# Experts computed only on rows sent to them, in one iteration with the attention of the same batch, in a fused audio-tower kernel

## The chip, the cores and the metric

The kernel runs on one core of a Trainium2 chip, all in fp32. The metric is device time in microseconds (us) from start to end of one execution; lower is better. The engines are called as the profile calls them: PE (TensorE, matmuls and transposes), DVE (VectorE), ACT (ScalarE), POOL (GpSimd) and SP (SyncE, which here issues the DMAs). Each has its own instruction queue and takes it strictly in order; they meet at semaphores.

## What is computed

The reference, cut to what matters, for x of 32 batches of 80000 samples:

```python
f = dct(frames_of_128(x))                         # 626 frames of 128 per batch (the last one is zero)
xo = concat(mamba2(f, fwd), flip(mamba2(flip(f), bwd))) @ proj_W.T + proj_b
h1 = layernorm(f + xo)                            # selective scan: 4 heads of 64, state 16, both directions

# what follows is wrapped in  h = h + block(layernorm(h)):
p = softmax(u @ gate_w + gate_b); top_w, top_idx = top_k(p, 2)                    # mixture of 8 experts
moe = sum_e gate[t, e] * (gelu(u @ w1[e] + b1[e]) @ w2[e] + b2[e])                # w1 128x512, w2 512x128
att = softmax over 8 following tokens of (q[t + w] + pos[w]) * k[t], times v[t + w]     # per channel
ffn = pattern FFN: top 64 of 512, then top 128 of 256, then top 64 of 512 activations kept
```

The gate is zero for the six experts that a token has not chosen.

## The kernel before, in words

A batch is 626 tokens, held as 5 tiles of 128 (`TILES`, `W` = 640). Three stages work on three different batches in one iteration of a loop: stage 1 (DCT, both Mamba2 directions, layer norm) on batch b, stage 2 (experts, then windowed attention) on b−1, stage 3 (the top-k FFN) on b−2. `run` writes two iterations ahead of the loop, 30 in it and two behind it. The order of the work inside an iteration is written out by hand: each engine has a string (`PE_ORDER`, `ACT_ORDER`, `DVE_ORDER`, `POOL_ORDER`), and each digit of it says whose stage's next step is emitted there; a step ends at a `yield`. SP has no string: per iteration it loads x, stores the output `hk` (L266, L267) and spreads the decays (L273, L279).

Stage 1 has 12 windows of 121 rows (6 chunks, 2 directions). For each, DVE runs a scan over the decays (L904) on a buffer of a ring of four (`ab0` to `ab3`), which SP fills from `decay_rows` in HBM by a broadcast load (L279), and multiplies (L912, L915); PE computes around it (L491, L501, L507, L527). At its end POOL does the last steps of the layer norm (L348, L311, L353, L356) and `h = h + u` (L359).

Stage 2 takes moments of h on DVE (L863, L866, L868, L869), POOL normalizes (L311, L316), PE and DVE compute the gate (L951 to L968). All eight experts then run on all 640 tokens, with their weights in SBUF for the whole program: 64 matmuls for the first layer (L574, each 128 hidden units by 320 tokens), ACT's gelu on each (L778), and 160 matmuls (L585) for the second, in 10 groups of four outputs. DVE first adds the product of gates and b2 (L973), then each output times its gate: 40 operations at L982. The attention follows: q, k, v on PE, eight products on DVE (L992), maxima (L995 to L998), POOL subtracts (L370), ACT exponentiates 128x5120 (L794), POOL sums trees (L376, L381, L385, L390, L399), DVE multiplies (L1003), takes a reciprocal (L1007) and the last product `kf` (L1010); PE transposes it, DVE adds it (L1013).

Stage 3 is DVE's largest: for every tile and each of three lists, rounds of MAX (eight largest, L1038) and MATCH_REPLACE (L1040), then masks (L1049, L1078), with PE's transposes and matmuls between; the last matmul of a tile (L682) is added to `hk` on DVE (L1060). `hk` is first filled with a copy of h by POOL (L408). Each first MAX on a1 waits for PE's matmul and ACT's gelu (L804) of that tile. Two tick instructions (L314, L1031) are 1 element wide.

PSUM has 8 banks of 128x512: `pS` (stage 1) three, `pM` (stage 2) three, `pD` (stage 3) two. Two small pieces show the form of the order:

```python
def merged(order, *stages):
    for digit in order:
        stage = stages[int(digit) - 1]
        if stage is not None:
            next(stage, None)
```

## Time and profile before

| | us |
|---|---|
| median of 3 runs | 8677.74 |
| lowest to highest | 8659.9 to 8679.93 |
| profiled execution, its own time | 8673.34 |
| its span | 8670.7 |
| PE busy | 6907.8 (80%) |
| DVE busy | 7915.2 (91%) |
| ACT busy | 3389.3 (39%) |
| POOL busy | 2524.6 (29%) |
| granted PE clock, mean | 0.809 of full speed |

Busy times are of one profiled execution, and the sum of a prediction is made against that execution's own time. The span counts from the first to the last instruction. DVE's share is a mean over the whole program; the loop has the same 262 us pattern 30 times, so one iteration, and the seam between two of them, can be read for all.

### The profile page before, as it was taken

How to read it: one execution, taken by the hardware profiler on the slowest of the kernel's cores; microseconds unless marked ns; L12 is line 12 of the kernel's file. 1: busy time of each engine (PE TensorE's matmuls, PEld its weight loads, DVE VectorE, ACT ScalarE, POOL GpSimd, SP SyncE). 2: the span in 40 equal slices, each digit the busy share in tenths (PEclk: the TensorE clock that was granted, in tenths of full speed). 3: DMA queues.
4: the chain of work that ended last, by engine and by line, in shares of the span. 5: the costliest groups of instructions: out<-in, count | busy, mean ns of one | idle time of the engine just before them, and what ended most of it. 6: DMA issues, size and time to landing. Idle time of an engine off the chain costs nothing.

```text
span 8670.7 us, 114685 instructions
## 1 busy us (share of the span) xinstructions
PE 6907.8 (80%) x35336; PEld 5042.4 (58%) x35336; DVE 7915.2 (91%) x23276; ACT 3389.3 (39%) x5803; POOL 2524.6 (29%) x2481
## 2 busy tenths in 40 slices
PE   6788887788878788878788887888878888777863
PEld 4566565566655565655565655566655656555642
DVE  2699999999999999999999999999999999999998
ACT  2344433344433344433344433444333444333431
POOL 1332123332133332233322233321233322333320
PEclk8788877788877788877888877888877888777875
DMA  1000000000000000000000000000000000000000
GB/s 57 15 17 15 8 12 17 17 17 15 7 13 17 17 16 14 10 13 17 17 15 10 10 17 17 17 15 8 12 17 17 17 15 7 13 17 17 14 2 3
DMA packets 95339, 128.48 MB, mean 15 GB/s; under 512 B 7600, under 2 KB 94096, under 8 KB 94096
## 3 DMA queue, kind: packets, MB, share of 16 engines
q1 hardware_dynamic: 94736, 120.71, 5.0%
q8 instruction: 345, 5.65, 0.3%
q14 instruction: 258, 2.11, 0.1%
HBM read 109.68 MB, written 11.01 MB: 14 GB/s over the span
## 4 chain that ended last, share of the span: by engine, by line
DVE 55%; PE 32%; issue 5%; POOL 4%; ACT 3%; DMA 1%; DVEq 0%; SPq 0%; POOLq 0%; ACTq 0%
DVE m L1038 17%; DVE work L1040 15%; PE pM L585 9%; PE pM L574 7%; DVE a L1040 4%; DVE ab L904 3%; PE pS L507 2%; DVE hid L992 2%; ACT hid L778 2%; DVE h L982 2%; PE pS L473 2%; DVE stats L863 2%; PE pS L501 2%; DVE a L1049 2%; PE pS L527 1%
## 5 line engine op out<-in xcount | busy, mean ns | idle before, releaser
L1040 DVE MATCH_REPLACE8 work<-m,work 128x256 f32<-128x256 f32 (+1 forms) x4192 | 2156.0, 522 | 0.0
L1038 DVE MAX8 m<-work 128x8 f32<-128x256 f32 (+1 forms) x4192 | 2014.0, 526 | 1.0
L574 PE MATMUL pM<-uT,cst 128*128 128x320 f32 x4096 | 1473.2, 480 | 179.5 <-DVE h L973 117.3
L311 POOL TENSOR_TENSOR rstd<-vare,mhalf 128x5 f32<-128x5 f32 x160 | 187.5, 1172 | 4671.2 <-DVE vare L869 4671.1
L778 ACT ACTIVATE hid<-pM,cst 128x320 f32<-128x320 f32 x2048 | 1061.6, 528 | 1031.2 <-PE pM L574 685.8
L585 PEld LDWEIGHTS pM<-cst,hid 128*128 128x128 f32 x10240 | 1191.9, 193 | 184.6 <-DVE h L982 110.8
L585 PE MATMUL pM<-cst,hid 128*128 128x128 f32 x10240 | 1219.2, 277 | 97.9 <-DVE h L982 97.2
L574 PEld LDWEIGHTS pM<-uT,cst 128*128 128x128 f32 x4096 | 690.5, 199 | 758.5 <-ACT hid L778 533.2
L473 PE MATMUL pS<-u_fm,wconv_s 128*128 128x315 f32 (+1 forms) x3072 | 861.3, 432 | 0.0
L507 PE MATMUL pS<-Mt,Xw 121*64 121x121 f32 x3072 | 377.9, 392 | 492.1 <-DVE Mt L915 492.1
L473 PEld LDWEIGHTS pS<-u_fm,wconv_s 128*128 128x128 f32 (+1 forms) x3072 | 496.1, 167 | 347.5 <-issue 92.9
L904 DVE TENSOR_TENSOR_SCAN ab<-ab,cst 121x488 f32<-121x488 f32 x384 | 614.4, 1606 | 32.3 <-DMA ab<-decay_rows 32.2
L370 POOL TENSOR_TENSOR hid<-hid,red 128x640 f32<-128x640 f32 x256 | 387.4, 1548 | 809.1 <-DVE red L998 809.1
L752 ACT COPY xs<-pS 128x242 f32<-128x242 f32 x384 | 138.9, 362 | 1171.5 <-PE pS L507 1171.5
L507 PEld LDWEIGHTS pS<-Mt,Xw 121*64 121x64 f32 x3072 | 245.9, 201 | 571.9 <-DVE Mt L915 526.8
L1038 DVE MAX8 m<-a 128x8 f32<-128x512 f32 x768 | 504.3, 677 | 38.4 <-issue 38.2
L982 DVE SCALAR_TENSOR_TENSOR h<-pM,lgt,h 128x128 f32<-128x128 f32 x1280 | 358.5, 343 | 130.7 <-PE pM L585 120.6
L399 POOL TENSOR_TENSOR hid<-hid 128x640 f32<-128x640 f32 x224 | 393.0, 1778 | 130.2 <-DVE hid L1003 125.1
L501 PE MATMUL pS<-xs,skip 128*128 128x121 f32 x1536 | 359.7, 379 | 14.7 <-ACT xs L752 14.7
L1040 DVE MATCH_REPLACE8 a<-m,a 128x512 f32<-128x512 f32 x512 | 345.3, 674 | 0.0
L677 PE MATMUL pD<-cst,a 128*128 128x128 f32 x640 | 146.4, 372 | 248.8 <-DVE a L1049 171.7
L831 ACT COPY selT<-pD 128x512 f32<-128x512 f32 x160 | 93.4, 584 | 638.8 <-PE pD L677 638.8
(195 smaller groups left out, 11986.4 us busy)
## 6 DMA issues: line engine op xcount, KB each, us to landing
ab<-decay_rows SPq DMA_DIRECT2D x384, 230.7 KB
x_sb<-in_x SPq DMA_DIRECT2D x32, 256.0 KB
out<-hk SPq DMA_DIRECT2D x32, 256.0 KB
cst<-in_weights SPq DMA_DIRECT2D x2, 2048.0 KB, 12.0
hid<-in_setup SPq DMA_DIRECT2D x1, 1904.0 KB, 20.9
out<-hk SPq DMA_DIRECT2D x32, 57.0 KB
x_sb<-in_x SPq DMA_DIRECT2D x32, 56.5 KB
cst<-in_weights SPq DMA_DIRECT2D x1, 1344.0 KB, 17.0
```

Source lines behind the costliest of these rows:

```text
L370: last = nc.gpsimd.tensor_tensor(lg[:, w, :], lg[:, w, :], red[:, 0, :], ALU.subtract)
L399: last = nc.gpsimd.tensor_tensor(lg[:, w, :], lg[:, w, :], lg[:, w + n, :], ALU.add)
L473: last = nc.tensor.matmul(pS[0:rows, 512 * (n % 3):512 * (n % 3) + HQ], wt, tap(d, i, half * HQ, HQ), start=(j == 0), stop=(j == len(block ...
L501: nc.tensor.matmul(pS[:, B2 + g * WIN:B2 + (g + 1) * WIN], skip[:, 2 * d + g, :], xs[d][:, g, NS + ch * WIN:NS + (ch + 1) * WIN], start=(g ...
L507: last = nc.tensor.matmul(pS[r * HD:(r + 1) * HD, B2 + g * WIN:B2 + (g + 1) * WIN], Xw[d][:, hh, :], Mt[d][:, hh, :], start=False, stop=(g ...
L574: nc.tensor.matmul(pM[:, 512 * (n % 2):512 * (n % 2) + W // 2], w1[:, e, j * P:(j + 1) * P], uT[:, lo:lo + W // 2], start=True, stop=True) ...
L585: last = nc.tensor.matmul(pM[:, B2 + P * (m % 4):B2 + P * (m % 4 + 1)], hid[:, e % 2, j, tok(t)], w2[:, e, j, :], start=(j == 0), stop=(j ...
L778: nc.scalar.activation(hid[:, e % 2, j, lo:lo + W // 2], pM[:, 512 * (n % 2):512 * (n % 2) + W // 2], ACT.Gelu, bias=c("b1")[:, n // 2:n / ...
L904: nc.vector.tensor_tensor_scan(decays, decays, c("scan_src", WIN), 0.0, ALU.mult, ALU.add).then_inc(G["scanned"].s, 1)
L982: last = nc.vector.scalar_tensor_tensor(h2[:, t, :], pM[:, B2 + P * (m % 4):B2 + P * (m % 4 + 1)], gate[:, t, e:e + 1], h2[:, t, :], ALU.m ...
L1038: link(nc.vector.max(m[i], now[i]), len(tiles) - 1)
L1040: link(nc.vector.match_replace(work[i], m[i], now[i], GONE), len(tiles) - 1 if r or firsts is None else 0)
```

## The change

Four stages with the lags 0, 1, 1 and 2: stage 2 is now routing and experts, stage 3 the attention **of the same batch in the same iteration**, stage 4 the top-k FFN. Three batches are in flight, as before. The experts run only on the rows sent to them:

1. DVE marks the two chosen experts of each token, PE counts with two matrices of constants (`before`, `ones`) how many earlier rows chose the same expert (`rank_ps`), and DVE makes of this a slot for each row, experts following one another in whole tiles of 128 rows, and the expert of each of the 17 tiles (`MT` = 2·5 + 8 − 1).
2. POOL scatters the normalized rows to `routed_rows` in HBM with ten indirect DMAs (L463), SP loads them back as tiles (L334) and reads the 17 expert numbers into registers (L372), with which it loads each tile's expert (w1, w2, b1, b2 in one DMA of 128x1156, 592 KB, L327) into a ring of three.
3. For each tile PE does 4 up matmuls, one for the bias, 4 down, and the transpose of the tile after the next; ACT does 4 gelus of 128x128 and a copy of answer and transpose together (`keep`). SP stores the answers to `answer_rows` (L341), POOL gathers them by ten indirect DMAs (L471), and DVE adds them to h2 into h3, times their weights, in ten operations (L1143, L1146).
4. SP gets an order of its own. The decay loads (L316), the expert loads and the row loads now stand in one queue.
5. Attention has a bank of its own, `pA`; `pM` shrinks to two. Its q, k and v go one after the other through that bank, and its transposes go in 4 + 1 tiles. h, h2 and h3 are separate buffers, as are un and u3. POOL's h2 = h + u (L453) waits for `moe_done` of the batch before, and the hk copy (L518) is moved to the end of the attention, directly ahead of it.
6. The experts' weights (4 MB) are not loaded ahead any more; `routed_rows` is zeroed once at the start.

The diff, cut to its core:

```diff
+MT = 2 * TILES + E - 1
+WR = 3
+EC = 4 * P + KB * P + KB + P
+STAGE_LAG = (0, 1, 1, 2)
...
-POOL_ORDER = ("321132222222221121111")
+POOL_ORDER = ("214211412131133333333331")
+SP_ORDER = ("1212122222222222311311222112212222122222244")
...
+        def sp_stage2(sp, b):
...
+            which = expert_of_tiles(sp)
+
+            def weights(i):
+                sp.wait_ge(G["tile_done"].s, G["tile_done"](b, max(i + 1 - WR, 0)))
+                sp.dma_start(expert[i % WR][:], experts_d[bass.ds(which[i], 1), :, :].rearrange("o p c -> p (o c)")).then_inc(G[f"expert{i % WR}"].s, 16)
...
+            for i in range(WR):
+                weights(i)
+            yield
+
+            sp.wait_ge(scattered.s, scattered(b, 160))
+            sp.wait_ge(G["moe_done"].s, G["moe_done"](b, 0))
+            routed(0)
+            routed(1)
+            for i in range(MT):
+                if i + WR < MT:
+                    yield
+                    weights(i + WR)
+                if i % 4 == 1 and i // 4 + 2 < GROUPS:
+                    yield
+                    routed(i // 4 + 2)
+                if i % 2 == 1 or i == MT - 1:
+                    yield
+                    answers(i // 2)
...
         def pool_stage2(pool, b):
+            normalized(pool, 1, 1, b, un, h2).then_inc(G["u2_done"].s, 1)
+            yield
+
+            pool.wait_ge(G["u2_done"].s, G["u2_done"](b, 1))
+            pool.wait_ge(G["slots_done"].s, G["slots_done"](b, 1))
+            nc.gpsimd.tensor_tensor(ticks[:, 0:1], zero1[:, 0, :], zero1[:, 0, :], ALU.add)
+            for k in range(2 * TILES):
+                nc.gpsimd.indirect_dma_start(routed_d, bass.IndirectOffsetOnAxis(ap=slot[:, k:k + 1], axis=0), un[:, k % TILES, :], None,
+                                             bounds_check=MT * P - 1, oob_is_err=False).then_inc(scattered.s, 16)
+            yield
+
+            pool.wait_ge(G["y_out0"].s, G["y_out0"](b, 80))
+            pool.wait_ge(G["y_out1"].s, G["y_out1"](b, 64))
...
+            for k in range(2 * TILES):
+                nc.gpsimd.indirect_dma_start(rows[:, k, :], None, answers_d, bass.IndirectOffsetOnAxis(ap=slot[:, k:k + 1], axis=0),
+                                             bounds_check=MT * P - 1, oob_is_err=False).then_inc(gathered.s, 16)
...
+            def up(i):
...
+                for j in range(KB):
+                    last = nc.tensor.matmul(pM[:, bank(i) + j * P:bank(i) + (j + 1) * P], w1_of(i, j), turned[:, (i + 2) % 4, 1, :],
+                                            start=True, stop=True)
+                last.then_inc(G["hid_ps"].s, 1)
+
+            def down(i):
...
+                nc.tensor.matmul(at, c("ones", 1), b2_of(i), start=True, stop=False)
+                for j in range(KB):
+                    last = nc.tensor.matmul(at, hid[:, i % 2, j, :], w2_of(i, j), start=False, stop=(j == KB - 1))
+                if i + 2 < MT:
+                    last = turn(i + 2)
+                last.then_inc(G["tile_done"].s, 1)
...
-                for m in range(4 * i, 4 * i + 4):
-                    e, t = divmod(m, TILES)
-                    last = nc.vector.scalar_tensor_tensor(h2[:, t, :], pM[:, B2 + P * (m % 4):B2 + P * (m % 4 + 1)], gate[:, t, e:e + 1],
-                                                          h2[:, t, :], ALU.mult, ALU.add)
...
+            for t in range(TILES):
+                last = nc.vector.scalar_tensor_tensor(h3[:, t, :], rows[:, t, :], top8[:, t, 0:1], h2[:, t, :], ALU.mult, ALU.add)
+            link(last)
+            for t in range(TILES):
+                last = nc.vector.scalar_tensor_tensor(h3[:, t, :], rows[:, TILES + t, :], top8[:, t, 1:2], h3[:, t, :], ALU.mult, ALU.add)
+            last.then_inc(G["moe_done"].s, 1)
```

**SP's queue from the output store or x on to the first decay loads.** In these rows buffer numbers are left out; a name in brackets is the semaphore waited for, and ISA or REGISTER_ALU rows are waits and registers. Before:

```order
L266 ISA [waits out_sb]
L266 DMA out<-hk 128x4x128
L267 ISA
L267 DMA out<-hk 114x128
L272 ISA [waits dA_sb]
L273 DMA decay_rows<-dAT 48x122 [waits scanned]
L279 DMA ab<-decay_rows 121x488 [waits m_done,dA_out]
L279 DMA ab<-decay_rows 121x488 [waits m_done] x3
```

After, the third expert load to the fourth tile's:

```order
L327 DMA expert<-in_experts 128x1156
L305 REGISTER_ALU
L306 ISA [waits dA_sb]
L307 DMA decay_rows<-dAT 48x122 [waits scanned]
L334 DMA rows<-routed_rows 128x4x128 [waits moe_done,scattered]
L334 DMA rows<-routed_rows 128x4x128
L316 DMA ab<-decay_rows 121x488 [waits m_done,dA_out]
L316 DMA ab<-decay_rows 121x488 [waits m_done] x3
L327 ISA [waits tile_done]
L327 DMA expert<-in_experts 128x1156
```

The two row loads and their wait for the scatters now stand between the decays' store and the first decay load, and expert loads stand among the decay loads; the output store has gone to the end of the iteration.

**DVE's queue at the seam between two iterations.** `ub_t` is stage 1's sum, `pD` the output of the FFN. Before:

```order
L866 BN_AGGR mv<-stats 128x2 [waits link1]
L866 BN_AGGR mv<-stats 128x2 x4
L868 TENSOR_SCALAR nmean<-mv 128x5 [waits link1]
L869 TENSOR_SCALAR vare<-mv 128x5
L1060 TENSOR_TENSOR hk<-hk,pD 128x128 [waits fin_ps,sel3]
L1060 TENSOR_TENSOR hk<-hk,pD 128x128 [waits fin_ps]
L1097 ISA
L301 COMPARE_AND_BRANCH
L863 BN_STATS stats<-h 128x6 [waits u4_done,h1_done]
```

After (`lg` is the attention's weighted values, `pA` its transposes, `h` here stands for h3 up to the branch):

```order
L1177 TENSOR_TENSOR kf<-lg,red 128x640 [waits val_tree]
L1180 TENSOR_TENSOR h<-h,pA 128x512 [waits attT_ps]
L1229 TENSOR_TENSOR hk<-hk,pD 128x128 [waits fin_ps,sel3]
L1184 TENSOR_TENSOR h<-h,pA 128x128 [waits attT_ps]
L1016 BN_STATS stats<-h 128x6 [waits h3_done]
L1021 TENSOR_SCALAR nmean<-mv 128x5 [waits link3]
L1022 TENSOR_SCALAR vare<-mv 128x5
L1229 TENSOR_TENSOR hk<-hk,pD 128x128 [waits fin_ps]
L380 COMPARE_AND_BRANCH
L1016 BN_STATS stats<-h 128x6 [waits h1_done]
```

Before, the last rows of an iteration were stage 1's, and the attention lay inside it; now the last product of the attention, its two additions and its moments come last, and the first rows of the next iteration take moments of h2 as before.

**POOL's queue at the same place, after.** `un` and `u` are normalized rows, `vare` the variances:

```order
L510 TENSOR_TENSOR lg<-lg 128x640 [waits val_tree]
L404 TENSOR_TENSOR rstd<-vare,mhalf 128x5 [waits var3]
L407 TENSOR_TENSOR tick_pool<-zero 128x1 [waits rstd3]
L409 TENSOR_SCALAR u<-h,nmean,rstd 128x128 x5
L517 ISA [waits h3_done]
L518 TENSOR_TENSOR hk<-h,zero 128x640 [waits out_dma]
L453 TENSOR_TENSOR h<-h,u 128x640 [waits moe_done,attn_scaled]
L380 COMPARE_AND_BRANCH
L404 TENSOR_TENSOR rstd<-vare,mhalf 128x5 [waits var2]
L407 TENSOR_TENSOR tick_pool<-zero 128x1 [waits rstd2]
L409 TENSOR_SCALAR un<-h,nmean,rstd 128x128 x5
L461 TENSOR_TENSOR ticks<-zero 128x1 [waits slots_done,u2_done]
L463 DMA routed_rows<-un,slot 2176x128 x10
```

Before, stage 1's layer norm and `h = h + u` ended POOL's iteration and the hk copy opened the next one, alone; now the attention's last sum, u4, the hk copy and h2 stand in a row, and the ten scatters (last row) follow behind the normalization.

## Rows read from the trace of the kernel before

**Rows 1.** The page's part 1: busy time and share of the span, xinstructions.
```profile
PE 6907.8 (80%) x35336; PEld 5042.4 (58%) x35336; DVE 7915.2 (91%) x23276; ACT 3389.3 (39%) x5803; POOL 2524.6 (29%) x2481
```

**Rows 2.** The page's part 4: the chain that ended last, by engine.
```profile
DVE 55%; PE 32%; issue 5%; POOL 4%; ACT 3%; DMA 1%; DVEq 0%; SPq 0%; POOLq 0%; ACTq 0%
```

**Rows 3.** Windows: length, busy time of each engine, PEclk, DMA share, GB/s.
```profile
608.00:4010.00 3402.00, 2787.32 (x14318) 2038.55 (x14316) 3201.41 (x9436) 1379.25 (x2350) 1016.50 (x995) 0.82 0.05 14
4272.00:8200.00 3928.00, 3212.47 (x16513) 2347.97 (x16514) 3695.38 (x10900) 1593.27 (x2712) 1174.56 (x1152) 0.82 0.05 14
```

**Rows 4.** Instructions of line L359, start and end of the span: min/median/max ns, starts in us.
```profile
L359 POOL TENSOR_TENSOR h<-h,u x3: 1530/1530/1533, 141.1 to 634.6; 128x640 f32<-128x640 f32 x3
...
L359 POOL TENSOR_TENSOR h<-h,u x3: 1532/1532/1533, 7718.0 to 8243.6; 128x640 f32<-128x640 f32 x3
```

**Rows 5.** Instructions of line L408.
```profile
L408 POOL TENSOR_TENSOR hk<-h,zero x32: 1248/1252/1257, 375.6 to 8489.7; 128x640 f32<-128x640 f32 x32
```

**Rows 6.** Timeline of DVE at the seam: start us, us, instruction [idle before <-releaser].
```profile
4041.55 0.29 DVE L1060 TENSOR_TENSOR hk<-hk,pD 128x128 f32<-128x128 f32 x1 [3.16 <-PE pD L682]
4046.27 1.07 DVE L863 BATCH_NORM_STATS2 stats<-h 128x6 f32<-128x128 f32 x5 [4.43 <-POOL h L359]
...
4048.77 0.69 DVE L1038 MAX8 m<-a 128x8 f32<-128x512 f32 x1 [0.68 <-issue]
```

**Rows 7.** Groups of DVE, 4010 to 4272: xcount | busy us, mean ns | idle before.
```profile
L904 DVE TENSOR_TENSOR_SCAN ab<-ab,cst 121x488 f32<-121x488 f32 x12 | 19.3, 1617 | 0.0
...
L982 DVE SCALAR_TENSOR_TENSOR h<-pM,lgt,h 128x128 f32<-128x128 f32 x40 | 11.2, 342 | 1.7 <-PE pM L585 1.5 <-DVE a L1049 0.2
...
L973 DVE TENSOR_TENSOR h<-h,pM 128x640 f32<-128x640 f32 x1 | 0.8, 810 | 0.0
...
L967 DVE TENSOR_TENSOR lgt<-lgt,top 128x40 f32<-128x40 f32 x2 | 0.4, 200 | 0.1
```

**Rows 8.** Instructions of line L904 (scans), first iteration and a steady one.
```profile
L904 DVE TENSOR_TENSOR_SCAN ab<-ab,cst x12: 1165/1168/1175, 78.0 to 109.0; 121x488 f32<-121x488 f32 x12
...
L904 DVE TENSOR_TENSOR_SCAN ab<-ab,cst x12: 1146/1563/2191, 4206.0 to 4265.7; 121x488 f32<-121x488 f32 x12
```

**Rows 9.** The page's part 5: PE groups.
```profile
L574 PE MATMUL pM<-uT,cst 128*128 128x320 f32 x4096 | 1473.2, 480 | 179.5 <-DVE h L973 117.3
...
L585 PE MATMUL pM<-cst,hid 128*128 128x128 f32 x10240 | 1219.2, 277 | 97.9 <-DVE h L982 97.2
...
L507 PE MATMUL pS<-Mt,Xw 121*64 121x121 f32 x3072 | 377.9, 392 | 492.1 <-DVE Mt L915 492.1
```

**Rows 10.** Windows of 10 us, PE alone: length, busy, PEclk, DMA share, GB/s.
```profile
3994.00:4004.00 10.00, 10.00 (x50) 0.50 0.29 79
...
4094.00:4104.00 10.00, 10.00 (x76) 1.00 0.00 0
```

**Rows 11.** The page's part 6: line, engine, xcount, KB each, us to landing.
```profile
cst<-in_weights SPq DMA_DIRECT2D x2, 2048.0 KB, 12.0
```

**Rows 12.** Waits of SP's queue: us in total, times, longest us.
```profile
SPq L279 <- DMA decay_rows<-dAT: 30.5, 32, 1.5
...
SPq L124 <- DMA out<-hk: 1.8, 1, 1.8
```

**Rows 13.** Timeline of SP's queue, first iteration.
```profile
74.39 1.49 SPq L279 DMA_DIRECT2D ab<-decay_rows  x4
```

**Rows 14.** Instructions of three POOL lines: min/median/max ns.
```profile
L314 POOL TENSOR_TENSOR tick_pool<-zero x160: 192/193/194, 45.4 to 8472.5; 128x1 f32<-128x1 f32 x160
...
L311 POOL TENSOR_TENSOR rstd<-vare,mhalf x160: 1164/1175/1192, 44.1 to 8471.2; 128x5 f32<-128x5 f32 x160
...
L348 POOL TENSOR_TENSOR rstd<-vare,mhalf x32: 1960/1960/1971, 127.8 to 8228.7; 128x10 f32<-128x10 f32 x32
```

**Rows 15.** Timeline of POOL, attention of one iteration.
```profile
3959.01 12.01 POOL L370 TENSOR_TENSOR hid<-hid,red 128x640 f32<-128x640 f32 x8 [25.43 <-DVE red L998]
...
4001.10 12.49 POOL L399 TENSOR_TENSOR hid<-hid 128x640 f32<-128x640 f32 x7 [4.12 <-DVE hid L1003]
4013.56 1.65 POOL L339 TENSOR_TENSOR yg<-xs,zs 128x525 f32<-128x525 f32 x2
```

485 lines of the change are left out of this document (290 added, 195 removed).

## The prediction

> **What bounds the kernel now.** I read the page first. VectorE (DVE) is busy 91% of the span, the matmul engine (PE) 80%, ScalarE (ACT) 39%, GpSimd (POOL) 29% [rows 1], and the chain that ended last runs 55% on DVE and 32% on PE [rows 2]. Two windows of whole steady iterations hold 3201.41 us of DVE work in 3402 and 3695.38 in 3928 [rows 3]: 94.1% busy. The loop's period comes from the starts of an instruction that runs once per iteration, POOL's h += u (L359): there are 29 periods between 634.6 and 8243.6 [rows 4], **262.4 us** each. So DVE works 246.9 us of an iteration and stands idle 15.5. The timeline of the seam between two iterations shows about half of that idle time: 3.16 us for the last output matmul, 4.43 for POOL's h, 0.68 more [rows 6], together 8.3; the other 7.2 lie in small waits. What the change is worth is what it does to these 246.9 and 15.5.
>
> **DVE work that goes and comes.** In one iteration [rows 7] the 40 accumulations of expert outputs (L982) are 11.2 us, the first sum with b2 (L973) 0.8, the two gate products (L967) 0.4. In come ten accumulations of L982's form, 2.8; eleven small operations for the slots and the expert table, at most 160 wide, at 0.2 to 0.25 each like L967's, 2.6; and 0.3 because h3's sum is split in two. Adding up all rows of the loop in both orders with the trace's durations gives −7.1: 246.9 becomes 239.8.
>
> **Scans.** The twelve scans are 19.3 us of an iteration [rows 7], each from 1.15 to 2.19; in the first iteration, where POOL does nothing beside them, all take 1.17 [rows 8]. Below, a DVE row's position is the sum of the durations of the rows ahead of it in the changed loop. The scans stand at positions 44 to 121, when POOL has issued its ten scatters and waits for the answers; its attention passes come later. I take 12 × (1.60 − 1.17) = 5.2 off: 234.6. The lower bound of this gain is nothing, should the indirect DMAs or the attention passes slow DVE wherever they land.
>
> **PE and ACT.** L574 and L585 took 1473.2 + 1219.2 us over 32 batches [rows 9], 84.1 per iteration. In their place stand 17 tiles of 10 matmuls or transposes of 128x128, at L585's 1219.2/5120 = 0.238 each: 40. DVE, not PE, sets the end, so I count none of the 44 as gain; it is slack. [...] One tile's expert is 592 KB; 2048 KB took 12.0 us [rows 11], so a load takes 3.5 to 5 us; 17 are 60 to 85 us of an iteration, three in flight. I cost them at nothing: the tiles' own PE time and the mixes between them cover that; without that cover each tile past the third would wait up to 2 us.
>
> **Waits that come.** (a) SP: the decay loads (L316) now stand behind the wait for all ten scatters. The slots are ready at DVE position 26.9. With p the price of one indirect DMA on POOL, scan 0 is ready at 26.9 + 10p + 2 (landing; 1.5 and 1.8 in [rows 12]) + 0.8 for two issues + 3.5 from a decay load's issue to its scan (74.39 [rows 13] to 78.0 [rows 8]) = 44.9 at p = 1.17, with the DVE at 43.8; with semaphores I say 2 us late.
> (b) POOL: the gather follows the last answers' store and must be in by position 154.8. It starts 12.7 us after the last combine; 5.3 us are left at p = 1.17, none at p = 1.7.
> (c) The trace has no indirect DMA. **p** is bounded by POOL's small instructions: 0.19 (128x1 add) below and 1.96 (pow on 128x10) above [rows 14]. I take 1.17, the pow on 128x5, as nearest to an instruction that reads one column of 128 and starts something for each. [...]
> (d) PE between expert tiles and mixes: both stand in its one queue. Mix 0 is ready near 75 and DVE is there at 72 to 73. Over the mixes, tiles 5 to 14 (10 × 2.23 at full clock) and twelve windows at 2.0 (L507 alone 377.9/384 = 0.98 at a mean clock of 0.8 [rows 9]) are 46 us of PE beside 45.8 of DVE. I charge 1. Idle inside the iteration: 7.2 + 2 + 1, about **10**.
> (e) The seam: a batch's attention now ends where the iteration does. kf waits for POOL's tree; that chain ran from 3959.01 to 4013.59 [rows 15], 54.6 us with its own waits, 45 to 50 of it work, against 46.4 of DVE work laid beside it: 3. The transposes into pA: 0.9. Then u4's moments, POOL's pow (1.17) and five scalings (1.1 to 2.2), PE's transposes, ACT's copy, a1's matmul, ACT's table and gelus stand in a row before the next iteration's first MAX: 11, with 2 of DVE work beside. POOL's hk copy (1.25) and h2 (1.53) queue there too, behind the store of the batch before (0.7 of issue, 1.8 of landing [rows 12]), 5.3 in all, hidden in those 11. Sum **13**, against 8.3.
>
> **Sum.** 234.6 + 10 + 13 = 257.6. A walk like this misses waits and invents none, so I add 1.4: **259** per iteration. The first iteration ended at 141.1 [rows 4], the second at 375.6 [rows 5]: I take 133 (4 MB of weights less to load ahead) and 226 (no experts' DVE work, 7 less). Iteration 32 took 8489.7 − 8243.6 = 246 and becomes 222, since nothing of experts and attention is left in it; the last stays near 183. With 2.6 around the span: 133 + 226 + 30 × 259 + 222 + 183 + 2.6 = **8537**, say 8540. The profiled run took 8673.34, 0.05% under the runs' median of 8677.74; no shift is made.
>
> **Rivals.**
> **A, slower**: an indirect DMA costs its upper bound. At p = 1.96 scan 0 is 7.9 us later and the gather 2.6 late: +10.5, 269.5 per iteration, 8852. It decides from a loss of 4.7 on, p about 1.64. For: sending 128 rows is more work than a pow on five columns. Against: an issue need not wait for its landing. Chance 0.22.
> **B, slower**: PE's work is now short bursts between three engines, and it is granted 0.50 where the expert part had 1.00 [rows 10]. The 46 us of (d) become 92, PE sets the pace there, and the period is near 300: 9700. For: the clock is at 0.50 in other parts. Against: PE has no longer gaps there than before. Chance 0.05.
> **C, no change**: in (d) each tile waits for ACT and each mix for DVE, in one queue; 0.4 us at each of twelve mixes is 5 per iteration, 8690. For: L507 already sat 492 us waiting for DVE's Mt [rows 9]. Chance 0.13.
> **D, faster**: waits overlap, and idle stays at 15.5: 250 per iteration, 8270. For: (a) and (e) take independent work beside them. Against: seam work is one chain. Chance 0.13.
> **E, it doesn't do what it says**: half of PE's work on experts goes and the time doesn't move, since the chain is 55% DVE's [rows 2]. That is how I read it, and it is in each case above: the gain comes from DVE's 12 us, not from PE's 44.
>
> **How the numbers follow.** Forecast 0.47, A 0.22, B 0.05, C 0.13, D 0.13. A measurement of this kernel tells about 0.3% (26 us) from no change. Faster by more: forecast, D and 0.02 of C, 0.62. Within: 0.10 of C. Slower: A, B and 0.01 of C, 0.28. The range runs from 8330 to 8890: it holds the forecast, C, A by rows, and the nearer half of D; B and the rest of D, some 0.15, are left out.
>
> **What would show it.** POOL's h2 (L453) at a period of 259 with DVE busy 234 to 236 of it; scans near 1.2; indirect DMAs 1.2 us apart; DVE waiting some 2 us for ab0; a seam idle near 13, behind kf, pA and a1. It would be wrong with DMAs 1.6 us apart or more and long waits for ab0 or the gather (A), with PEclk 0.5 between scan 0 and scan 11 (B), with waits of 0.4 us or more at every mix (C), or with DVE's work not falling.

## The result, and the profile after

The changed kernel takes 8774.64 us (median of 4 runs, 8771.2 to 8786.13) beside 8678.83 for the kernel before (4 runs, 8659.9 to 8688.26): a ratio of **1.0117**, 95% interval 1.0103 to 1.0132. It is slower by 1.2%, where 1.6% faster was forecast. The profiled run took 8773.84 us, its span 8771.9. One execution of e15_head_early (below) took 10598 us at a mean granted clock of 0.533; it lies outside the range given there and outside the ratio.

The page's busy time by engine, answering to [rows 1]:

```profile
PE 6056.2 (69%) x31240; PEld 4389.9 (50%) x31240; DVE 7622.0 (87%) x22604; ACT 3284.6 (37%) x6696; POOL 2994.0 (34%) x3187
```

The change does what it says: DVE's work fell by 293 us (7915.2 to 7622.0) and PE's by 852. The time rose by 96, so DVE stands idle longer. The chain that ended last, answering to [rows 2], shows DMA and POOL where PE had been:

```profile
DVE 60%; PE 13%; DMA 9%; issue 8%; POOL 7%; ACT 2%; SPq 1%; POOLq 0%; DVEq 0%; ACTq 0%
```

**The period.** POOL's h2 (L453) runs once per iteration:

```profile
L453 POOL TENSOR_TENSOR h<-h,u x32: 1530/1532/1543, 134.3 to 8338.8; 128x640 f32<-128x640 f32 x32
```

The first two starts are 134.3 and 372.9, the third 638.7; (8338.8 − 638.7)/29 is 265.5 us per iteration, forecast 259, before 262.4. Two windows inside the loop, answering to [rows 3] (length, then busy time of PE, PEld, DVE, ACT, POOL, then PEclk, DMA share, GB/s):

```profile
700.00:4094.00 3394.00, 2389.34 (x12479) 1737.18 (x12477) 3046.89 (x9022) 1308.82 (x2662) 1193.32 (x1260) 0.75 0.22 65
4360.00:8300.00 3940.00, 2804.40 (x14582) 2035.28 (x14582) 3538.03 (x10524) 1544.04 (x3129) 1371.00 (x1461) 0.75 0.22 66
```

These windows are not whole numbers of iterations. Over the 29 whole ones (length, DVE busy, PEclk, DMA share, GB/s):

```profile
638.70:8338.80 7700.10, 6901.02 (x20474) 0.75 0.22 65
```

6901.02 / 29 is **238.0 us of DVE work in an iteration, and 27.5 us idle**. Before it was 246.9 and 15.5. So 8.9 us of work went and 12.0 of idle time came.

**Where DVE waits.** DVE's waits over the same 29 iterations of both kernels (what waited, for what: us in total, times, longest). After, 639 to 8339:

```profile
DVE ab L1057 <- DMA ab<-decay_rows: 227.5, 87, 6.0
DVE stats L1016 <- POOL h L453: 176.3, 29, 6.3
DVE stats L1016 <- ACT h L837: 163.8, 29, 7.4
DVE kf L1177 <- POOL lg L510: 41.5, 29, 1.4
DVE hk L1229 <- PE pD L814: 38.6, 29, 1.5
DVE h L1180 <- PE pA L741: 37.1, 29, 1.3
DVE Xw L1065 <- PE pS L602: 34.1, 34, 3.0
```

Before, 635 to 8243:

```profile
DVE stats L863 <- POOL h L359: 121.3, 29, 4.7
DVE hk L1060 <- PE pD L682: 99.3, 29, 4.0
DVE h L982 <- PE pM L585: 45.5, 63, 1.2
DVE m L1038 <- issue: 34.5, 29, 2.1
...
DVE ab L904 <- DMA ab<-decay_rows: 0.8, 2, 0.4
```

In these rows "issue" stands where the trace shows nothing that the engine waited for. Divide by 29. Scans waiting for their decays went from 0 to **7.8 us** per iteration, at three scans of twelve (87 waits in 29 iterations); the wait for h2 from 4.2 to 6.1; the wait for the next batch's h (L837) is new, **5.6**. kf, pA and hk together are 4.0, hk alone was 3.4. That is 16 us more. In return the small waits of the list before are nearly gone, among them 1.6 for the expert matmuls (L982 <- PE) and 1.2 for the first MAX (L1038). The difference is the 12 us.

**The seam** in DVE's timeline at 4085, answering to [rows 6] (start, us, instruction, idle before):

```profile
4085.04 0.69 DVE L1180 TENSOR_TENSOR h<-h,pA 128x512 f32<-128x512 f32 x1 [1.28 <-PE pA L741]
...
4089.90 0.29 DVE L1229 TENSOR_TENSOR hk<-hk,pD 128x128 f32<-128x128 f32 x1 [1.47 <-PE pD L814]
4096.12 1.07 DVE L1016 BATCH_NORM_STATS2 stats<-h 128x6 f32<-128x128 f32 x5 [5.93 <-POOL h L453]
...
4103.30 1.07 DVE L1016 BATCH_NORM_STATS2 stats<-h 128x6 f32<-128x128 f32 x5 [5.36 <-ACT h L837]
```

With 1.4 for kf and 0.4 for L1184 that is 15.8 idle, where the forecast had 13. POOL's and PE's rows say why:

```profile
4089.95 2.18 POOL L409 TENSOR_SCALAR u<-h,nmean,rstd 128x128 f32<-128x128 f32 x5
4093.34 1.25 POOL L518 TENSOR_TENSOR hk<-h,zero 128x640 f32<-128x640 f32 x1 [1.21 <-DMA out<-hk]
4094.55 1.53 POOL L453 TENSOR_TENSOR h<-h,u 128x640 f32<-128x640 f32 x1
```

```profile
4092.18 1.12 PE L750 MATMUL pA<-cst,u 128*128 128x128 f32 x4 [2.32 <-POOL u L409]
4094.05 0.47 PE L754 MATMUL pA<-cst,u 128*128 128x128 f32 x1 [0.75 <-ACT u4T L950]
4098.12 1.32 PE L545 MATMUL pS<-cst,x_sb 128*128 128x128 f32 x5 [3.59 <-DMA x_sb<-in_x]
```

u4 is ready at 4092.13. POOL waits 1.21 for the out store, copies hk, and only then adds h2. PE turns u4, comes to the loop's end, and 3.59 us later turns the *next* batch's x; ACT copies it, PE does the DCT, ACT copies h, and DVE goes on at 4103.30. The forecast had put the adding of h2 inside the 11 us of a1's chain, and had no term for h.

**The scans and the masks.** DVE's groups from 700 to 8300, shapes kept apart. After:

```profile
L1057 DVE TENSOR_TENSOR_SCAN ab<-ab,cst 121x488 f32<-121x488 f32 x347 | 405.7, 1169 | 221.5 <-DMA ab<-decay_rows 221.5
L1218 DVE SCALAR_TENSOR_TENSOR a<-work,a 128x512 f32<-128x512 f32 x228 | 219.2, 961 | 5.7
L1247 DVE SCALAR_TENSOR_TENSOR a<-work,a 128x256 f32<-128x256 f32 x145 | 80.9, 558 | 0.0
```

Before:

```profile
L904 DVE TENSOR_TENSOR_SCAN ab<-ab,cst 121x488 f32<-121x488 f32 x348 | 560.7, 1618 | 0.8 <-DMA ab<-decay_rows 0.8
L1049 DVE SCALAR_TENSOR_TENSOR a<-work,a 128x512 f32<-128x512 f32 x230 | 157.8, 686 | 5.8
L1078 DVE SCALAR_TENSOR_TENSOR a<-work,a 128x256 f32<-128x256 f32 x145 | 60.5, 417 | 1.0
```

A scan fell from 1618 to 1169 ns, 5.4 us per iteration against 5.2 forecast. But the masks that read two tiles now stand beside POOL: 686 became 961 ns (2.2 us per iteration), 417 became 558 (0.7). At 4077.83 and 4079.62 L1218 took 1.73 and 1.89 us while POOL's tree (L510) ran beside it; of its 256 instructions 62 took over 0.9 us, and every one of them lay beside L510.

**The indirect DMAs** in POOL's timeline:

```profile
4130.77 0.97 POOL L463 DMA_INDIRECT routed_rows<-un,slot  x1 [0.30 <-issue]
4132.05 0.97 POOL L463 DMA_INDIRECT routed_rows<-un,slot  x1 [0.31 <-issue]
```

These are the second and third of ten. They stand 1.28 us apart (the first, at 4129.35, 1.42 ahead), near the 1.17 taken and far from rival A's 1.64. The gathers stand 1.31 apart and land 2.6 after issue.

### The profile page after: what moved, and what is told of

Same layout as the page of the kernel before. It is cut to its first block, busy times and chain, and to the rows that moved or that the text cites. A ratio compares the mean times of both kernels' runs of the same rounds, so it can differ in the third digit from the quotient of the medians.

```text
span 8771.9 us, 110100 instructions
## 1 busy us (share of the span) xinstructions
PE 6056.2 (69%) x31240; PEld 4389.9 (50%) x31240; DVE 7622.0 (87%) x22604; ACT 3284.6 (37%) x6696; POOL 2994.0 (34%) x3187
## 4 chain that ended last, share of the span: by engine, by line
DVE 60%; PE 13%; DMA 9%; issue 8%; POOL 7%; ACT 2%; SPq 1%; POOLq 0%; DVEq 0%; ACTq 0%
DVE m L1207 19%; DVE work L1209 19%; DMA ab<-decay_rows 5%; POOL lg L510 4%; DVE a L1209 3%; DVE lg L1159 2%; POOL routed_rows L463 2%; PE pM L704 2%; PE pM L693 2%; DMA x_sb<-in_x 2%; PE pS L584 1%; DVE ab L1057 1%; DVE Mt L1068 1%; DVE stats L1016 1%; DVE lg L1170 1%
## 5 line engine op out<-in xcount | busy, mean ns | idle before, releaser
L584 PE MATMUL pS<-u_fm,wconv_s 128*128 128x315 f32 (+1 forms) x3072 | 974.7, 470 | 41.3 <-ACT Cs L868 40.8
L906 ACT ACTIVATE hid<-pM,expert 128x128 f32<-128x128 f32 x2176 | 622.7, 371 | 384.2 <-PE pM L693 382.3
L1057 DVE TENSOR_TENSOR_SCAN ab<-ab,cst 121x488 f32<-121x488 f32 x384 | 449.0, 1169 | 295.8 <-DMA ab<-decay_rows 295.7
L704 PE MATMUL pM<-expert,hid 128*128 128x128 f32 x4352 | 652.4, 295 | 0.0
L693 PE MATMUL pM<-turned,expert 128*128 128x128 f32 x4352 | 602.2, 283 | 40.8 <-ACT turned L915 38.1
L481 POOL TENSOR_TENSOR lg<-lg,red 128x640 f32<-128x640 f32 x256 | 383.5, 1536 | 662.0 <-DVE red L1165 662.0
L693 PEld LDWEIGHTS pM<-turned,expert 128*128 128x128 f32 x4352 | 539.6, 194 | 89.9 <-issue 64.5
L704 PEld LDWEIGHTS pM<-expert,hid 128*128 128x128 f32 x4352 | 545.9, 197 | 67.3 <-issue 3.1
L510 POOL TENSOR_TENSOR lg<-lg 128x640 f32<-128x640 f32 x224 | 362.6, 1643 | 160.9 <-DVE lg L1170 155.7
L814 PE MATMUL pD<-cst,selT 128*128 128x128 f32 x1280 | 328.4, 437 | 108.0 <-ACT selT L984 108.0
L814 PEld LDWEIGHTS pD<-cst,selT 128*128 128x128 f32 x1280 | 281.7, 324 | 171.4 <-ACT selT L984 171.4
L471 POOL DMA_INDIRECT rows<-answer_rows,slot x320 | 323.6, 1011 | 105.0 <-issue 105.0
```

What stands on the lines that cost most here:

```text
L471: nc.gpsimd.indirect_dma_start(rows[:, k, :], None, answers_d, bass.IndirectOffsetOnAxis(ap=slot[:, k:k + 1], axis=0), bounds_check=MT * P ...
L481: last = nc.gpsimd.tensor_tensor(lg[:, w, :], lg[:, w, :], red[:, 0, :], ALU.subtract)
L510: last = nc.gpsimd.tensor_tensor(lg[:, w, :], lg[:, w, :], lg[:, w + n, :], ALU.add)
L584: last = nc.tensor.matmul(pS[0:rows, 512 * (n % 3):512 * (n % 3) + HQ], wt, tap(d, i, half * HQ, HQ), start=(j == 0), stop=(j == len(block ...
L693: last = nc.tensor.matmul(pM[:, bank(i) + j * P:bank(i) + (j + 1) * P], w1_of(i, j), turned[:, (i + 2) % 4, 1, :], start=True, stop=True)
L704: last = nc.tensor.matmul(at, hid[:, i % 2, j, :], w2_of(i, j), start=False, stop=(j == KB - 1))
```

## The experiments

All edits are to the changed kernel, and ratios are to the kernel before, timed on the same chip. Waits are totals of DVE from 700 to 8100, about 28 iterations. The theory at the start was that three waits ate the gain, each made by the order of a queue. So three orders were moved, one at a time and together. Where a time "after L453" is given, it is the median over the 29 iterations of that run's trace.

**e1_x_early.** SP loads the next x before it waits to store out.

```diff
-SP_ORDER = ("1212122222222222311311222112212222122222244")
+SP_ORDER = ("142121222222222223113112221122122221222222")
-            run(sp, SP_ORDER, sp_stage1, sp_stage2, idle, sp_stage4)
+            run(sp, SP_ORDER, sp_stage1, sp_stage2, idle, sp_stage4, lags=(0, 1, 1, 3))
```

> SP loads x of the next batch ahead of the output store, as before the change, and not behind it. Theory (x sits behind a store that waits for the iteration's last DVE operation): DVE's wait for ACT's h (L837), 5.6 us per iteration, falls to under 2.5, the rest being POOL's h2 that ACT's copy of x waits for; the period falls from 265.5 by 3 to 5.5, the time by 90 to 165 us to 8610-8685. Rival (the wait only moves to the first MAX or to scan 0, because the seam is bound by POOL's h2 and the decays come late anyway): period within 1 of 265.5, time within 30 of 8775.

8842.2 us, 1.0183 [1.0165, 1.0201]. The theory fell: DVE's wait for h stayed at 5.7 us per iteration. The trace also shows something the edit can't cause: engines stood before instructions for which nothing was missing, as `ACT xs L871 <- remote` for up to 6.3 us, and single register operations of SP of up to 0.71.

**e2_decays_first.** SP issues the decay loads ahead of the wait for scattered rows (the fourth and fifth step of its order):

```diff
-SP_ORDER = ("1212122222222222311311222112212222122222244")
+SP_ORDER = ("1211222222222222311311222112212222122222244")
```

> On SP the four first decay loads go ahead of the wait for the scatters and of the two row loads. Theory (queue order makes scan 0 late): the wait for ab0, 3 to 4.6 us in an iteration, falls to under 1, the period by 2.5 to 4, the time by 75 to 120 us to 8655-8700; the waits for later decays (some 3 us per iteration) stay. Rival (it is the traffic of the expert loads, which come out of the queue just ahead): ab0's wait stays over 2.5 and the time within 40 of 8775.

8992.0, 1.0356 [1.0339, 1.0373]. This theory fell too: DVE's scans still wait, and a new wait stands behind them.

```profile
DVE ab L1057 <- DMA ab<-decay_rows: 232.4, 82, 7.0
...
DVE tick L1200 <- ACT a L964: 120.3, 19, 7.6
DVE best L1207 <- ACT a L964: 49.9, 8, 7.9
```

The expert rows now leave SP behind the decays. PE's queue has the first tile's transposes ahead of the feed-forward matmuls (L772, L780) that make `a` for ACT's L964; the tile starts 61.5 us after L453 instead of 52.3, and DVE's top-k waits for `a`. The edit was not tested alone, though: in this run, as in e1, the last decays are copied 50.9 us after L453 and not 45.9, so that the first decay load left at 52.5, later than the 50.1 that it was to beat. e14 repeats the order without that delay.

**e3_h2_first.** POOL adds h2 ahead of the hk copy.

```diff
-POOL_ORDER = ("214211412131133333333331")
+POOL_ORDER = ("214211412131133333333133")
```

> POOL adds h2 = h + u in the gap ahead of u4 and not behind the copy to hk. Theory: DVE's wait for h2 at the seam, 6.1 us, goes, but x is loaded as late as before, so that the wait for h (L837) grows from 5.6 to 9 to 11 and the gain is only 0.5 to 2 us per iteration, 15 to 60 us: 8715-8760. Rival (the seam is POOL's h2 alone): the whole 6 us are gained, period 259.5, 8595.

8879.2, 1.0225 [1.0208, 1.0242].

```profile
DVE stats L1016 <- ACT h L837: 232.6, 27, 10.0
DVE stats L1016 <- issue: 78.0, 27, 3.1
```

The wait for h2 is gone, and the same idle time stands before the next thing: 8.6 us per iteration for h and 2.9 of "issue", 11.5 together, as much as both waits had been. The 2.9 is DVE's own loop end, which the wait for h2 had covered. Here, too, scans wait 284.5 us in all, with no edit near them: this run is of e1's set, and has its stalls.

**e4_all_three.** The three edits together.

> The three edits together. Theory: the waits are in different places of one chain per iteration, and x early together with h2 early frees both seam waits: 5.6 + 4 of 6.1 + 3.5 at ab0, 10 to 13 us per iteration of which the first MAX's wait takes back 2 to 4: period 255 to 257.5, time 8450 to 8530, below the kernel before (8679) by 1.7 to 2.6%. Rival (what is freed at the seam comes back at the decays, the gather and PE's mixes): period 260 or more, 8600 or more.

9028.7, 1.0397 [1.038, 1.0415]. No part had paid, and the three together did not either.

**e5_control.** The changed kernel unedited, among the next set of runs.

> The changed kernel, unedited, once more. Theory (the four edits really made it slower, by 2.5 to 8.5 us per iteration, because engines stalled on their next instructions around the first expert loads, which the first run of this kernel did not show): period 265.5 and 8775 again, within 0.3%, with no wait of that kind on ACT's L871. Rival (such stalls come and go with the load of a program or the session, whatever the edit): over 8810, with stalls of up to 6 us on ACT L871 and SP's first expert load 42 us or more after h2 and not 39.

8768.7, 1.0109 [1.0092, 1.0126], period 265.5, none of e1's stalls. The result repeats. Its scans wait 212.5 us in all; DVE waits 170.1 for h2 and 156.8 for h. These are the base of the comparisons below.

**e6_thin_experts.** Is it the experts' traffic that makes decays late? This kernel loads 128 of an expert's 1156 columns and leaves out the rest, so the experts' values are not those of the reference.

```diff
-                sp.dma_start(expert[i % WR][:], experts_d[bass.ds(which[i], 1), :, :]...
+                sp.dma_start(expert[i % WR][:, 0:P], experts_d[bass.ds(which[i], 1), :, 0:P]...
```

> Each expert load brings only the first 128 of its 1156 columns, 64 KB for 578 KB; the rest of w1 and all of w2 and the biases are left at zero, so the experts' values are left out; every instruction, wait and order stays. Theory (queue order and PE's half-clock projections make the decays late, not traffic): the wait for ab falls by 1 to 2.5 of 7.8 us per iteration since loads land a little faster, the seam's 6.1 and 5.6 stay, time 8700 to 8745. Rival (17 x 578 KB per iteration are what delays decay loads, row loads and answers): the wait for ab falls under 3 and the time to 8640 or less.

8732.5, 1.0072 [1.0055, 1.0089].

```profile
DVE ab L1059 <- DMA ab<-decay_rows: 163.1, 58, 5.0
```

The scans' wait falls from 212.5 in 83 places to 163.1 in 58, 7.6 to 5.8 per iteration, and the period from 265.5 to 263.9. The experts' traffic costs less than 2 us, and none of it at scan 0, which starts 55.8 us after L453 in both. From the first decay load to scan 0 it is 5.6 us in both as well; where the decay loads leave ahead of the two row loads it is 3.5 (e2) to 3.9 (e14). So the 2 us on top of the 3.5 forecast are the two row loads of 256 KB that leave just ahead.

**e7_pool_busy.** Thirty adds of 128x640 on POOL beside the scans.

```diff
+            for k in range(30):
+                pool.wait_ge(G["spare_done"].s, G["spare_done"](b, k))
+                nc.gpsimd.tensor_tensor(spare[:], ..., ALU.add)...
```

> POOL does 30 additions of 128x640 to a spare buffer behind the scatters, beside the scans and where it was idle. Theory (the scans are 1.17 and not 1.62 us only because POOL is idle beside them): the scans that fall beside these additions, 8 to 10 of 12, take 1.5 to 2.2 us, mean 1.45 to 1.65 over all; DVE's work rises by 3.5 to 6 us per iteration, the time by 80 to 250 us. Rival (scans are short because they stand singly between other DVE work, or for where the buffers lie): mean stays 1.17 and the time within 30.

8867.0, 1.0226 [1.0209, 1.0243]. The page's group of scans:

```profile
L1061 DVE TENSOR_TENSOR_SCAN ab<-ab,cst 121x488 f32<-121x488 f32 x384 | 521.8, 1359 | 202.1 <-DMA ab<-decay_rows 202.1
```

1169 became 1359 ns by POOL's work alone, less than the 1450 expected, because only a third of the scans lay beside an added POOL instruction: those 129 took 1.72 us in the mean, the 253 clear of it 1.17. That POOL's quiet makes scans short is shown. The masks pay the same price here (L1218 of the changed kernel, 960 ns in e5):

```profile
L1222 DVE SCALAR_TENSOR_TENSOR a<-work,a 128x512 f32<-128x512 f32 x226 | 306.7, 1357 | 5.7
```

DVE's MAX of 128x512, which reads one tile, is not stretched: 0.68 us beside the added instructions and clear of them.

**e8_all_three_thin.** e4 with e6's loads.

> The three edits of the fourth run, with the thin expert loads (experts' values left out). Theory (what the three edits lost they lost to stalls of SP, ACT and PE on their next instructions beside the burst of three expert loads): without the burst the stalls go, and the seam and the order give what was expected: period under 262, time under 8650, below both e6 and e4 by over 1%. Rival (the row loads behind the decays and the order itself are the loss, 4.6 us at the first MAX after scan 0): within 1% of e4, over 8930.

8889.2, 1.0249 [1.0232, 1.0266], no stalls. The scans' wait is down to 56.4 (2.1 per iteration), and the waits for `a` (L966 there) are 103.0 + 95.5, 7.3 per iteration. So the wait before the top-k that e2 brought is the order of the rows, neither the experts' traffic nor stalls: behind the four decay loads the first row load lands 7.0 us after its issue, here with thin experts as in e2 with whole ones, and 2.8 in the changed kernel.

**e9_x_early_again.** e1's kernel, unchanged, in another set of runs.

> The first experiment's kernel once more, since the control ran without any stall on instructions while the four edited kernels of the earlier set all had them. Theory (the stalls belong to that set of runs, or to where the programs lay then, and not to the edit): no register operation of SP over 0.2 us, first expert load 39 us after h2, decays from ACT at 46 us, period 265 to 265.6, time 8755-8785: no gain, since PE's first matmul after the loop's jump starts at 3.4 us either way. Rival (the edit shifts the code, and the stalls come with it): 8820 to 8850 again with SP's slow register operations up to 0.7 us.

8778.0, 1.0114 [1.0097, 1.013], with no stalls. e1's extra 64 us belonged to its set of runs, and e2 to e4 ran in that set: their ratios overstate, their waits' places stand. x early gains nothing by itself. PE's wait before L545 changes its name only, from the x load to "issue":

```profile
PE pS L545 <- issue: 100.4, 28, 4.9
```

That is 3.6 us per iteration for PE's jump to the loop's head.

**e10_x_and_h2.** e1's and e3's edits.

> x loaded ahead of the store and h2 added ahead of u4, the decay loads as in the changed kernel. Theory: from DVE's last output addition to its moments of h there are now 5.9 + 1.9 + 5.4 us; with x and h2 both ready, what is left is the jump of the loop (2.9 us on DVE, 3.4 on PE) and PE's two steps and ACT's two copies behind it, some 9 us, so the seam's idle falls by 3 to 4 us: period 261.5 to 263, time 8650 to 8700. Rival (DVE's h waits for PE's jump and u4's transposes, which follow DVE's last addition as before): period over 264.5, time over 8740.

8819.6 (8780.7 to 8824.8), 1.0151 [1.0122, 1.018]. The seam's idle time stays (238.4 for h, 77.5 "issue", 11.7 us per iteration), so the rival held: what h waits for is PE's place in its queue and the jump. The time is even 42 us above e9's in the medians, and the trace says where from. DVE's work is 239.3 us per iteration instead of 238.0, all of it in one instruction, kf (824 ns in e9):

```profile
L1177 DVE TENSOR_TENSOR kf<-lg,red x32: 825/2137/2141, 363.9 to 8615.6; 128x640 f32<-128x640 f32 x32
```

h2 added early is added beside kf, at 31 of 32 kfs. e3, e12 and e15 pay these 1.3 us too.


**e11_hint.** The jump back at the loop's end is announced by one more instruction in each engine's loop; the trace calls it BRANCH_PREFETCH_HINT and puts it at the head (39 ns on DVE).

```diff
-            with engine.Fori(last, NB) as b:
+            with nc.Fori(last, NB, engines=[engine.engine], hint_back_edge=True) as b:
```

> [...] Theory (a part of the seam is the jump itself, 3.4 us on PE ahead of its first matmul on x, and 2.9 on DVE): PE's jump hides nothing of x's load, which lands at the same time, so the gain is only 0 to 1 us per iteration: 8735-8775. Rival (the jump is hidden anyway or the announcement does nothing): the same within 15 us; and if it moves the code so that stalls come, 8800 or more.

8749.2, 1.008 [1.0063, 1.0096], against 1.0114 for e9 among the same runs. DVE's rows of the loop's end, from 700 to 8100, in this run:

```profile
L380 DVEq COMPARE_BRANCH  x28: 77/77/78, 897.6 to 8060.1; - x28
L380 DVEq BRANCH_PREFETCH_HINT  x28: 39/39/39, 898.2 to 8060.7; - x28
```

In the changed kernel:

```profile
L380 DVEq COMPARE_BRANCH  x28: 72/72/72, 903.4 to 8073.1; - x28
L380 DVEq FUSED_REGOPS  x28: 51/51/51, 906.5 to 8075.9; - x28
```

From the branch to DVE's next row it is 2.9 us there (median of 30) and 0.5 here. How the hint does that no trace shows. The wait for h is 140.8 instead of 157, that for h2 stays (175.2).

**e12_x_h2_hint.** e10 and e11.

> x early, h2 early and the jump announced, together. Theory (after x and h2 the jump is the seam's next limit): DVE goes to h2's moments within 0.5 us and PE starts on x within 1 us of the jump, so the seam loses 3 us more than with x and h2 alone: period 258.5 to 260.5, time 8560 to 8620, 0.7 to 1.4% below the kernel before. [...]

8731.7 (8706.9 to 8738.2), 1.0051 [1.0032, 1.0071].

```profile
DVE stats L1016 <- ACT h L837: 223.6, 28, 11.3
...
DVE stats L1016 <- issue: 16.7, 28, 0.6
```

DVE's jump goes from 2.9 to 0.6 us, PE's from 3.6 to 0.8. Against e10 the seam's idle time falls by the 3 us expected (11.7 to 8.6), and the time by 88. But e10 had not brought its own part: against the changed kernel 43 us are gained where 155 to 215 were expected, since h itself is still last, 8.0 per iteration.

**e13_decays_unit4.** The decays are computed and copied four at a time, so the last is ready sooner (`DA_UNIT = 8` becomes `4`).

> PE transposes the decays after 4 half projections and not after 8, some 8 us earlier, and ACT copies them as much earlier; SP's queue stays. Theory (two things hold scan 0 at the same time: the decays, copied at 45.9 us after h2, and on SP the wait for the scatters and two row loads, 49 to 50): alone it gains little, ab0's first load goes out at 49.5 to 50.2 as before, because the scatters end at 47.7: time 8745-8785, within 0.3% of 8770. Rival (the decays alone hold it): scan 0 2 to 4 us earlier, 8640 to 8710.

8779.1, 1.0115 [1.0092, 1.0139]. The last copy ends 40.8 us after L453 instead of 45.9, as expected without a gain: the first decay load still leaves at 50.4 (50.1 before), for it stands behind the wait for the scatters and SP's first row loads.

**e14_unit4_decays_first.** With e2's order too.

> The same, and on SP the first four decay loads ahead of the wait for the scatters. Theory: the decays' store goes out at 38 to 41 us and the loads by 43, before the scatters end (47.7), so the row loads aren't delayed and the loss of the second experiment (PE and ACT behind late rows, 7 us at the first MAX on a2) does not come; ab0's wait, 4 us, goes: period 261 to 262.5, time 8630 to 8690. Rival (DVE's time is given back at the mixes, PE being behind in order): the wait for Xw or for a later decay grows by as much, time over 8740.

8828.9, 1.0179 [1.0162, 1.0195].

```profile
DVE tick L1200 <- ACT a L964: 120.4, 19, 7.6
DVE ab L1057 <- DMA ab<-decay_rows: 98.2, 70, 3.0
DVE best L1207 <- ACT a L964: 55.1, 9, 7.3
```

Scan 0 comes at 51.3 instead of 55.8 and the scans' wait is halved (7.6 to 3.6 per iteration). The earlier copy alone (e13) gave nothing; what the earlier place on SP gives alone no undisturbed run shows. And 6.5 us come back before the top-k: the row loads, now second, land 6.8 us after their issue instead of 2.8, and the first tile starts at 56.5 instead of 52.3. Nor do the decays gain all that was open: their store leaves at once behind three whole expert loads, and SP waits for its landing.

```profile
SPq L316 <- DMA decay_rows<-dAT: 161.3, 27, 7.2
```

That is 6.0 us per iteration (1.2 in e2, where the store left some 6 us behind the last expert load). In e13 the wait for the scatters covers it.

**e15_head_early.** On PE and ACT the next batch's transposes and DCT stand ahead of the attention's last transposes, as a stage with lag −1; with e12's edits.

```diff
-PE_ORDER = ("14414442211112...
+PE_ORDER = ("4444422111121...
-            run(pe, PE_ORDER, pe_stage1, pe_stage2, pe_stage3, pe_stage4)
+            run(pe, PE_ORDER, pe_stage1, pe_stage2, pe_stage3, pe_stage4, pe_head, lags=(0, 1, 1, 2, -1))
```

> PE transposes x and does the DCT of the next batch ahead of the attention's last transposes, in the iteration before, and ACT copies h there; x is loaded and h2 added early, and the jump is announced. Theory (h was held by PE's queue: u4's transposes, then the jump, then x): DVE's wait for h falls from 8 to 11 (with x and h2 early) to under 1.5 us, and what the first MAX on a1 waits comes forward, 2 to 4 us; net 4 to 7 us off the seam: period 259 to 261.5, time 8560 to 8650. Rival (the seam is bound by u4's own chain: moments, POOL, PE, ACT, PE, ACT, as the prediction put it with 11 us): the whole wait moves to the first MAX and the period stays at 263 or more, 8710 or more.

8702.3 (median of 8 runs, 8672.6 to 8711.1), **1.0024** [1.001, 1.0038]: the best version, still 0.1 to 0.4% behind the kernel before.

```profile
DVE m L1213 <- issue: 188.5, 28, 7.5
```

The wait for h is gone. In its place DVE's first MAX stands 6.7 us per iteration before a1. The trace calls it "issue"; what ends just before is the u4 chain (POOL's scalings, PE's transposes, ACT's copies, a1's matmul, ACT's table load of 1.28 us and its gelus). This is the chain of forecast (e), now bare. DVE's idle time is 23.2 us per iteration here, 4.3 less than in the changed kernel, and of the 96 us that the change lost this version gives back some 70. So that much of the loss was the seam: the order there and the jump (the hint alone is worth 29, e11 against e9).

**e16_everything.** e15 and e14.

> Both: the early head of stage 1, and decays after 4 half projections with their loads first. Theory: the two gains lie in different stretches of DVE's chain and add up, 8 to 11 us per iteration: period 255 to 258, time 8440 to 8540, 1.6 to 2.7% below the kernel before. Rival (PE's work between is what binds, 46 us of tiles and mixes in one queue, and it takes back what comes early): period 261 or more, over 8620.

8766.3, 1.01 [1.008, 1.012]. The scans' wait is 98.4, but the wait for `a` (L970 there) is 182.2, and the first MAX waits 196.0.

**e17_ffn_before_rows.** e14, and PE's and ACT's order so that the feed-forward's matmuls and activations go ahead of the first tile (PE `2412224` to `4142222`, ACT `24224` to `44222`).

> The fourteenth run's kernel (decays after 4 half projections, their loads first), and on PE and ACT the top-k FFN's transposes, matmul and gelu for a2 of the first tile stand ahead of the first transposes of routed rows and not behind. Theory (in-order queues: PE waits for rows with the FFN's work behind it): DVE's wait for ACT's a (6.4 us per iteration) goes to under 1, period 262 to 263.5, time 8640 to 8700, on a par with the kernel before. Rival (the tiles start later by as much, and the mixes, which follow them on PE, hand it back through Xw and the gather): time over 8740.

8794.2, 1.0141 [1.0126, 1.0156].

```profile
DVE ab L1055 <- DMA ab<-decay_rows: 99.0, 71, 2.9
DVE tick L1198 <- ACT a L962: 85.1, 20, 7.3
```

With the part counted at `best`, the wait for `a` is 120, 4.3 per iteration of the former 6.5. So the order on PE and ACT explains a third of it; what else holds `a` was not settled. The first tile starts as late as in e14 (56.2 us after L453).

**e18_everything_ffn_before_rows.** e16 with e17's orders.

> The sixteenth run's kernel (early head, x and h2 early, announced jump, decays early) with that reordering. Theory: it loses its 6.5 us at a2 and keeps the rest: period 257.5 to 259.5, time 8550 to 8610, 0.7 to 1.4% below the kernel before. Rival (PE's queue hands it back): over 8660, no gain on the kernel before.

8731.9, 1.0067 [1.0052, 1.0081]. The scans wait 99.1, `a` 147, the first MAX 178.8; it is behind e15. No version tried beats the kernel before.

## Why the prediction was wrong

The forecast had DVE's work fall by 12.3 us per iteration and its idle time rise by 8.9. The work fell by 8.9 and the idle time rose by 12.0, so the period rose. Four steps failed: the wait for the decay loads (a), the seam (e), the masks' missing term in DVE's work, and the ends.

**DVE's work: a step that failed, by a missing term.** The forecast was 234.6 us per iteration, and 238.0 were measured: 3.4 too much, 102 us over 30 iterations. The scans gave 5.4 (5.2 taken). Missing was the other side of the same fact: POOL's passes left the scans and came to stand beside the masks that read two tiles, 2.9 us per iteration. e7 shows it on scans (1.17 and 1.72 us) and masks alike. The prediction priced what POOL leaves and not what it comes to stand beside. The rest, about 0.5 us, was not traced.

**(c) the indirect DMA: right.** 1.28 us apart for p = 1.17; rival A (p from 1.64) falls. Ten scatters took 12.6 us, from 4129.35 to 4141.97, and the gathers of 64 KB left 1.31 us apart and landed 2.6 us after their issue, so that none waited for the landing of the one ahead.

**(a) the decay loads: the step that failed most.** 2 us were taken, and 7.8 stand there. For scan 0 the walk's order was right and its sizes low: in the iteration shown, the first scatter is issued at 4129.35, the last ends at 4141.97 (12.6 us for 11.7), SP loads the first rows at 4143.26 and issues the decay loads at 4144.37, and scan 0 starts at 4149.45, 5.1 us later (5.6 in the median; 3.5 taken, and the difference is the two row loads just ahead, as e2 and e14 show). DVE had been there 4.03 us. But scan 0 is half of it. The scans of that iteration wait 7.0 us at three places: the walk looked at the first load alone, and the later ones stand in SP's queue too, behind expert loads that wait for their buffer (SP waited 57 us in 13 places at L327). The fifth decay load, whose buffer scan 0 had left free, was issued at 4186.44, and its scan waited 0.91 us; the last scan waited 2.08. e6 shows what the experts' traffic itself adds, 1.8. And taking the scatters away would not have helped much alone: the decays themselves are late, the last copy ending 45.9 us after L453. PE's projections ahead of them run at a granted clock of 0.50; how much of the lateness that makes no run shows. So two things hold scan 0 at nearly the same time. e13 takes away one and gains nothing, e14 takes away both and gains 4.5 us there, which the late rows take back.

PE's windows of 8 us after L453 at 4094.5 (length, busy, PEclk, DMA share, GB/s):

```profile
4110.50:4118.50 8.00, 6.92 (x28) 0.50 0.00 0
4118.50:4126.50 8.00, 8.00 (x23) 0.50 0.00 0
...
4134.50:4142.50 8.00, 8.00 (x30) 1.00 0.75 274
```

**(e) the seam: wrong by 2.8, and wrong in kind.** 13 idle forecast, 15.8 measured, by waits that the text called hidden. The 1.4 for kf (3 taken) and 1.3 for pA (0.9) were fair. The mistake is "hidden in those 11": the hk copy and h2 are not beside the u4 chain; DVE itself waits for h2 (6.1 us). And the next batch's transposes stand behind u4's in PE's one queue, with a loop end between them; nobody asked what the first instruction of the next iteration waits for. e3, e10 and e12 show that these waits lie on top of one another: remove one and the next is bare. Only with e15, which takes all of them away, does the u4 chain appear, at 6.7.

**(b) and (d): fair in the loop.** The gather has no wait in the loop's list. The waits of Xw for PE are 1.2 per iteration against 1 charged and 0.8 before; C's 0.4 at each mix is not there, nor is B's clock. From scan 0 on to behind scan 11 the granted clock was 1.00 (length, busy time of PE, PEld, DVE, ACT, POOL, then PEclk, DMA share, GB/s):

```profile
4149.45:4230.00 80.55, 77.46 (x548) 62.90 (x548) 77.27 (x222) 47.52 (x117) 1.86 (x3) 1.00 0.50 149
```

PE's work fell by 26.6 us per iteration, not 44. The 2.23 for a tile at the full clock is what the kernel before shows: from 4094 to 4104 the 32 records of L585 are 3.73 us, 0.112 apart, two to a matmul. 7 of the missing 17 are the tiles, 47.3 us per iteration where 40 were taken; beside them the mean clock went from 0.82 to 0.75 [rows 3]. It was slack, as said.

**The ends: 42 us too low, a step that failed.** The first iteration ended at 134.3 (133 forecast) and the last took 188.4 (183). But the second took 238.6 (226), and iteration 32, to hk's copy, 244.7 for 222. "Nothing of experts and attention is left in it" was misread: the last batch's stages 2 and 3 run in it, and its gather has nothing beside it.

```profile
DVE h L1143 <- DMA rows<-answer_rows,slot: 19.5, 1, 19.5
```

**The sum.** 30 iterations × 6.5 over is 195, plus 42 at the ends: 237, the whole distance from 8537 to 8774. Of the 6.5, 3.4 is DVE's work, and 3.1 is idle time (27.5 against 24.4, to which the forecast rounded 24.6). Inside the idle time (a) is 5.8 too low and (e) 2.8. The rest, 3.9 us, was put at 9.6 (7.2 carried over from before, 1 for (d), 1.4 added), though of the 7.2 some 1.7 were waits for the expert matmuls that the change removes [rows 7]. That the sum missed by no more is luck: 5.7 us too much for small waits stood against 8.6 too little for the two large ones. The added 1.4 rested on no row.

**The chances.** 0.28 was given to slower and the range to 8890 holds the time. The place was rival A's (late decays), but the price was not the DMA's, so that the range was right for a cause that it did not hold.
